# Picking expert outputs with a 0/1 product and combining on four row tiles, in a decoder layer on one core

## Time and profile before

| | us |
|---|---|
| median of 3 runs (2023.99 to 2030.28) | 2028.57 |
| the profiled execution | 2031.14 |
| its span, first to last instruction | 2029.3 |
| stage of experts in the trace, first DMA issue to first DMA issue of `combine` | 1841.07 to 1984.94 |
| `combine` in the trace, to the end of the span | 1984.94 to 2029.3 |
| busy over the whole span: PE / DVE / ACT / POOL | 87% / 63% / 42% / 27% |

### The profile page before, as it was taken

The page is one execution under the profiler, slowest core; times in us unless marked ns, Lnnn a source line. Parts: engine busy times, 40 slices in busy tenths (PEclk is TensorE's granted clock), DMA queues, the critical chain, the costliest instruction groups (busy, mean ns, idle before and its releaser), DMA issues. The chain is left out here.

```text
span 2029.3 us, 48825 instructions
## 1 busy us (share of the span) xinstructions
PE 1767.7 (87%) x19756; PEld 847.4 (42%) x19756; DVE 1268.6 (63%) x2435; ACT 858.0 (42%) x1031; POOL 543.2 (27%) x650
## 2 busy tenths in 40 slices
PE   3799999999998398999999989999999999976566
PEld 2556666666655222343343333333433333322224
DVE  4666666677663477867867777678678678821005
ACT  0333244333322114645645645545456546551213
POOL 0535455545512705014032041140140310000002
PEclk7899999999997669999999999999999999987775
DMA  5200000000000220211111201101111013145982
GB/s 180 81 24 3 24 24 24 3 24 24 3 13 3 64 96 2 70 45 45 38 36 49 69 1 62 56 25 48 45 49 48 22 49 131 75 176 211 421 372 97
DMA packets 64439, 143.62 MB, mean 71 GB/s; under 512 B 11376, under 2 KB 34448, under 8 KB 56048
## 3 DMA queue, kind: packets, MB, share of 16 engines
q1 hardware_dynamic: 59504, 136.29, 18.5%
q10 hardware_dynamic: 4736, 4.46, 0.7%
HBM read 97.59 MB, written 4.98 MB: 51 GB/s over the span
## 5 line engine op out<-in xcount | busy, mean ns | idle before, releaser
L1558 DVE TENSOR_REDUCE mx<-cpsV 128x1 f32<-128x512 f32 x1024 | 651.3, 684 | 228.0 <-PE cpsV L1261 214.1
L1462 ACT ACTIVATE w<-cpsA 128x1024 f32<-128x1024 f32 x512 | 496.2, 1021 | 373.7 <-PE cpsA L1329 373.6
L1261 PE MATMUL cpsV<-w 96*128 96x512 bf16 x1024 | 339.7, 403 | 63.2 <-DVE mx L1558 49.1
L1283 PE MATMUL cacc<-w 128*32 128x512 f32 x2048 | 281.1, 614 | 0.4 <-ACT w L1462 0.4
L1329 PE MATMUL cpsA<-w 99*128 99x512 bf16 x1024 | 276.9, 393 | 0.3
L1261 PEld LDWEIGHTS cpsV<-w 96*128 96x128 bf16 x1024 | 84.8, 99 | 376.9 <-DVE mx L1558 216.2
L1119 POOL TENSOR_TENSOR w<-w,zero 128x1024 bf16<-128x1024 f32 x21 | 39.7, 1892 | 645.1 <-ACTq L1435 645.1
L654 ACT COPY QK<-psA 128x1024 f32<-128x1024 f32 x64 | 64.8, 1012 | 252.2 <-PE psA L466 252.2
L1329 PEld LDWEIGHTS cpsA<-w 99*128 99x128 bf16 x1024 | 99.1, 100 | 128.2 <-ACT w L1462 11.8
L466 PE MATMUL psA<-xt,wq 128*128 128x512 f32 x256 | 133.3, 645 | 19.0 <-DMA xt<-in_xT 13.0
L744 POOL TENSOR_TENSOR VP<-V,VPF 128x128 f32<-128x128 f32 (+2 forms) x256 | 128.0, 531 | 45.7 <-PE psA L479 41.2
(11 more groups left out here) (214 smaller groups left out, 2396.5 us busy)
## 6 DMA issues: line engine op xcount, KB each, us to landing
w<-in_w SPq DMA_DIRECT2D x64, 1024.0 KB, 17.9
w<-w SPq DMA_DIRECT2D x192, 128.0 KB, 2.3
w<-w SPq DMA_DIRECT2D x192, 64.0 KB, 2.0
w<-in_ctxT SPq DMA_DIRECT2D x8, 1024.0 KB, 5.0
pro_xt<-in_xT SPq DMA_DIRECT2D x8, 512.0 KB, 7.0
x_tok<-in_x SPq DMA_DIRECT2D x8, 512.0 KB, 9.1
xtv<-in_xT SPq DMA_DIRECT2D x8, 512.0 KB, 5.0
xt<-in_xT SPq DMA_DIRECT2D x8, 512.0 KB, 4.5
```

What stands on the lines that cost most here:

```text
L1261: nc.tensor.matmul(out, Qst[q // 2][0:ROWS, hh, g * P:(g + 1) * P], Kst[q // 2][0:ROWS, hh, half * BANK:(half + 1) * BANK], start=True, st ...
L1283: last = nc.tensor.matmul(acc[BLK * jj:BLK * (jj + 1), :], Vc[:, c, 4 * q + jj, :], Pr[:, (2 * s + jj // 2) % 4, (jj % 2) * T:(jj % 2 + 1) ...
L1462: nc.scalar.activation(Pr[:, (2 * s + pp) % 4, :], src, ACT.Exp, scale=CA_SCALE).then_inc(act_evac, 1)
L1558: nc.vector.tensor_reduce(mx[:, q % 2, row, k % 2:k % 2 + 1], full(m[k]), AX_X, ALU.max).then_inc(dve_evac, 1)
```

## The change

`experts` and `combine` become one stage, `experts_and_combine`, written out without hardware loops. Weights, products, Gelu and the order inside a group stay; what differs:

1. `o_scratch` is gone, and so are the four DMAs per group, ACT's wait for them, the reload of `oall` and the barrier between the stages. Instead PE picks the rows: after the w1 product of group n it computes `pick_rows(n-1)`, eight products of a 0/1 table (`pick`, a new input of 128 x 480 fp32) with `og` of the group before, contraction over 128 partitions, 32 x 256 outputs each, accumulated over all groups in bank 7 (`psS`). Row tile j gets sequences j and 4+j, experts in partitions 32j to 32j+31.
2. DVE adds b2 from `psS` into `oall` (two instructions of 128 x 256) after the last pick.
3. The combination runs in 16 units of 256 tokens (half a sequence, one PSUM bank each), four units per `combine(s)`: eight products with 32 contraction rows, the four of one `g` in the four row tiles 0, 32, 64, 96 and in four banks.
4. For six of the units (`X_BY_PE`) PE first writes the tokens into the bank by a product with the identity (`add_x`), DVE only takes statistics from PSUM, and ACT normalizes straight from PSUM. Two of these `add_x` stand before the w2 product of the last group, four between `combine(1)` and `combine(2)`. For the other ten units DVE adds the tokens as before.
5. b1, `pick`, four copies of b2 and all eight p8 tiles are loaded at the stage's start, 14 DMAs in all; before its first w1 product PE waits for `c_loaded`, that is for `pick` and the four b2 copies, the last of which is the twelfth DMA in SP's order.
6. The w2 weights of the last group come in eight DMAs of half size, and its product waits for each half apart.
7. The output of all units has its own place in SBUF, over the first w1 buffer; SP issues the 16 output DMAs, two units at a time.

```diff
-def experts(nc, sh, dram):
+UNITS = 2 * B
+BT = 4
+def pick_table():
+    q, c = np.arange(P)[:, None, None], np.arange(2 * E - EG)[None, None, :]
+    b = np.arange(B)[None, :, None]
+    return ((q % BLK == b) & (c == E - EG + q // BLK)).astype(np.float32).reshape(P, -1)
+def experts_and_combine(nc, sh, dram, out):
...
+        psB, psS = ps[:, 5, :], ps[:, 7, :]
+        UNIT_BANKS = (5, 6, 0, 1), (2, 3, 4, 7)
+        def unit(u):
+            return BT * (u // 8) + u % BT, u // BT % 2, ps[:, UNIT_BANKS[u // BT % 2][u % BT], :]
+        X_BY_PE = (0, 1, 8, 9, 10, 11)
         @block.sync
         def _(sp):
             sp.dma_start(b1r[:], dram["w1"][:, D, :]).then_inc(b_loaded, 16)
-            sp.dma_start(sh.b2[:], dram["w2"][:, F, :]).then_inc(sh.b2_loaded, 16)
...
+            sp.dma_start(pick[:].rearrange("p b c -> p (b c)"), dram["pick"]).then_inc(c_loaded, 16)
+            for j in range(BT):
+                rows = slice(E * j, E * (j + 1))
+                sp.dma_start(b2[rows], dram["w2"][:, F, :]).then_inc(c_loaded, 16)
+                for h in range(2):
+                    t0 = (BT * h + j) * T
+                    sp.dma_start(p8[rows, h, :], sh.p8_dram[:, t0:t0 + T]).then_inc(p_loaded, 16)
+            for n in range(2, GROUPS):
+                sp.wait_ge(h_full, n - 1)
+                load_group_weights(sp, sh, dram, 1, n % 2, n * EG)
+                sp.wait_ge(o_full, n - 1)
+                if n < GROUPS - 1:
+                    load_group_weights(sp, sh, dram, 2, n % 2, n * EG)
+            for c0 in range(2):
...
+                    sp.dma_start(w2[n % 2][:, j, cs, :], src[:, cs, :]).then_inc(w2_part[c0], 16)
+            for u in range(UNITS):
+                sp.wait_ge(y_ready, u // 2 + 1)
+                sp.dma_start(out[b]...[:, 2 * half:2 * half + 2, :], y[:, u]).then_inc(saved, 16)
         @block.tensor
+            def pick_rows(n):
+                pe.wait_ge(o_evac, n + 1)
+                for h in range(2):
+                    for j in range(BT):
+                        last = nc.tensor.matmul(psS[E * j:E * (j + 1), h * D:(h + 1) * D],
+                                                pick[:, BT * h + j, E - EG - EG * n:2 * E - EG - EG * n], og[n % 2][:], ...)
+            def add_x(u):
+                for g in range(2):
+                    nc.tensor.matmul(bank[:, g * D:(g + 1) * D], sh.ident[:], sh.x[:, G * b + 2 * half + g, :], ...)
+            def combine(s):
+                for g in range(2):
+                    for j in range(BT):
+                        last = nc.tensor.matmul(bank[:, g * D:(g + 1) * D], p8[rows, b // BT, t0:t0 + P], oall[rows, b // BT, :], ...)
+            pe.wait_ge(c_loaded, 16 * (1 + BT))
+            for n in range(GROUPS):
+                (w1 product)
+                if n:
+                    pick_rows(n - 1)
+                (transposes)
+                if n == GROUPS - 1:
+                    for u in (0, 1):
+                        add_x(u)
+                (w2 product; in the last group waiting for w2_part[0], then w2_part[1])
+            pick_rows(GROUPS - 1)
+            combine(0)
+            combine(1)
+            for u in (10, 11, 8, 9):
+                (wait until unit u - 8 is out of the bank)
+                add_x(u)
+            combine(2)
+            combine(3)
         @block.scalar
-                    act.drain().then_inc(o_evac, 1)
-                    for j in range(EG):
-                        act.dma_start(sh.o_dram[...], og[n][BLK * j:BLK * j + B, :]).then_inc(o_saved, 16)
-                    act.wait_ge(o_saved, it * 128 + (n * 64 + 64 + 32))
+                if n >= 2:
+                    act.wait_ge(picked, n - 1)
+                nc.scalar.copy(og[n % 2][:], psO[n % 2]).then_inc(o_evac, 1)
         @block.vector
+            for h in range(2):
+                nc.vector.tensor_tensor(oall[:, h, :], psS[:, h * D:(h + 1) * D], b2[:], ALU.add).then_inc(oall_ready, 1)
+            for u in range(UNITS):
+                if u not in X_BY_PE:
+                    nc.vector.tensor_tensor(y[:, u], src, sh.x[...], ALU.add).then_inc(summed, 1)
+                dve.drain()
+                (2 bn_stats, drain, 2 bn_aggr)
```

More of the change, by code:

```diff
@@ L1672, in experts @@
         w2 = [t[:].rearrange("p (e c d) -> p e c d", e=EG, c=FC) for t in sh.w2]
+        y = sh.w1[0][:].rearrange("p (u g d) -> p u g d", u=UNITS, g=2)
         b1r, b1T = sb("b1r", [E, F]), sb("b1T", [P, FC, E])
@@ L1707, in _ @@
             pool.drain().then_inc(zeroed, 1)
[L1708 to L1713, removed]
+            for n in range(GROUPS):
+                if n >= 2:
+                    pool.wait_ge(h_full, n - 1)
+                nc.gpsimd.tensor_copy(mg4[n % 2][:, :, :, 0:B], sh.mT[:, :, EG * n:EG * (n + 1), :]).then_inc(mg_ready, 1)
@@ new lines, in add_x @@
+            def add_x(u):
+                b, half, bank = unit(u)
+                for g in range(2):
+                    nc.tensor.matmul(bank[:, g * D:(g + 1) * D], sh.ident[:], sh.x[:, G * b + 2 * half + g, :],
+                                     start=(g == 0), stop=False, skip_group_check=True)
+            def combine(s):
+                for g in range(2):
+                    for j in range(BT):
+                        u = BT * s + j
+                        b, half, bank = unit(u)
+                        t0, rows = (2 * half + g) * P, slice(E * j, E * (j + 1))
+                        last = nc.tensor.matmul(bank[:, g * D:(g + 1) * D], p8[rows, b // BT, t0:t0 + P], oall[rows, b // BT, :],
+                                                start=(u not in X_BY_PE), stop=True, skip_group_check=True)
+                last.then_inc(full, 1)
@@ new lines, in _ @@
+            for v in range(UNITS // 2):
+                act.wait_ge(rstd_ready, v + 1)
+                for u in (2 * v, 2 * v + 1):
+                    _, _, bank = unit(u)
+                    for g in range(2):
+                        src = bank[:, g * D:(g + 1) * D] if u in X_BY_PE else y[:, u, g, :]
+                        at = 2 * u + g
+                        last = nc.scalar.activation(y[:, u, g, :], src, ACT.Identity, bias=shift[:, at:at + 1],
+                                                    scale=rstd[:, at:at + 1])
+                last.then_inc(y_ready, 1)
@@ new lines, in _ @@
+            for u in range(UNITS):
+                b, half, bank = unit(u)
+                if u % BT == 0:
+                    dve.wait_ge(full, u // BT + 1)
+                src = bank.rearrange("p (g d) -> p g d", g=2)
+                if u not in X_BY_PE:
+                    nc.vector.tensor_tensor(y[:, u], src, sh.x[:, G * b + 2 * half:G * b + 2 * half + 2, :], ALU.add
+                                            ).then_inc(summed, 1)
+                    src = y[:, u]
+                dve.drain()
+                for g in range(2):
+                    nc.vector.bn_stats(stats[:, g, :], src[:, g, :])
+                dve.drain()
+                for g in range(2):
+                    last = nc.vector.bn_aggr(mv[:, u, g, :], stats[:, g, :])
+                if u % 2:
+                    last.then_inc(var, 1)
@@ L1917, in decoder_layer @@
             cross_attention(nc, sh, dram)
-            sh.b2 = weights.enter_context(nc.sbuf_tensor("b2", [E, D], F32))
-            sh.p8 = [weights.enter_context(nc.sbuf_tensor(f"p8_{n}", [E, T], F32)) for n in range(2)]
-            sh.b2_loaded = weights.enter_context(nc.semaphore("b2_loaded"))
-            sh.p8_loaded = [weights.enter_context(nc.semaphore(f"p8_loaded_{n}")) for n in range(2)]
-            experts(nc, sh, dram)
-            combine(nc, sh, dram, out)
+            experts_and_combine(nc, sh, dram, out)
 def _heads_inner(w):
```

245 lines of the change are left out of this document (91 added, 154 removed).

## The result

| | before | changed |
|---|---|---|
| median, us | 2028.8 (4 runs) | 2013.28 (4 runs, 2010.51 to 2016.96) |
| ratio, 95% interval | | 0.9929 (0.9905 to 0.9953) |
| forecast | | 2018.8, range 2012 to 2028 |
| profiled span | 2029.3 | 2008.8 |
| the stage: first DMA issue of the experts to the end of the span | 188.2 | 176.2 |

The changed kernel is faster by 15.5 us in the medians, more than the 9.8 us forecast. The two profiles differ by 20.5 us, but 8.5 of them lie ahead of the stage, in code that the change does not touch: the first DMA of the experts is issued at 1841.07 before and at 1832.61 after. It is 12.0 us shorter.

What follows compares the result with a forecast made beforehand. The weight stream bounds the experts, chains over engines the combination. End 1983.5 + 3.3 + 24.9 + 7.9 = 2019.5 against 2029.3, -9.8 us; from the median 2028.57 that gives 2018.8 us, range 2012 to 2028.

Steps and rivals of the forecast that it cites:

- rival D: Start costs little and PE stays hot: start +2, last group 11.6 us, -14.5 us in all, 2014.1 us; 16%.
- late start of the stream: At the stage's start PE's first w1 product waits for the twelfth DMA, moving the whole weight stream by 4.0 us.
- DVE's units: In the combination, ten units with an addition at 1.83 us, six without at 1.10: 24.9 us instead of 29.7.
- tail: After DVE's last unit, POOL, ACT and the output DMAs take 7.9 us, as before.
- Groups 0 to 6 at zero: DRAM wait goes, 16 short pick instructions per group come; both lie under the weight stream: 0 us.
- Group 7: Last group, from landing of w1 to end of w2 product: 14.3 us against 16.05, w1 product cold at 6.3.
- Half-size w2 at zero: Last group's half-size w2 transfers end four us before the second half is read: 0 us unless below half rate.
- Way to the first unit: From the last w2 product through og copy, picks, b2 addition and combine(0): 3.25 us instead of 10.4.
- Combine steps: Four row tiles overlap: sixteen instructions of combine(s) take 1.3 us first and 2 later, when PE is colder.
- Rival A: Row tiles do not run side by side: each combine(s) costs 7.0 us, PE bounds the end, 2034.6 us; 7%.
- B: Cold last group and late start eat the gain: start +5, last group 18 us, combine(2) late by 2, 2025.5; 22%.
- C: Late instruction fetch under the full stream, in the last group or the combination, costs 6 us: 2024.8 us; 10%.

Runs made afterwards that it cites:

- defer_c: Changed kernel with PE's wait for the table and b2 moved from ahead of the first w1 product to the first pick; stage 172.8 us, ratio 0.9899.
- before_lag: Kernel before, ACT's wait for the four DMAs to DRAM moved ahead of the copy that overwrites the same og buffer; stage 187.5 us, ratio 0.9996.
- scratch_writes: Changed kernel with the 32 small DMAs of og rows to DRAM put back beside the picks, read by nobody; stage 176.3 us, ratio 0.9942.
- warm2: Changed kernel with ten idle products on PE during its wait for the last w1 weights; stage 174.6 us, ratio 0.9931.
- whole_w2b: Changed kernel with the last group's w2 in four whole transfers, PE waiting for all; stage 176.2 us, ratio 0.9914.
- dram_trip: Changed kernel without the picks: og goes through DRAM and four DMAs bring it back, no barrier; stage 182.7 us, ratio 0.9950.
- x_by_dve: Changed kernel with X_BY_PE empty, so DVE adds the tokens for all 16 units; stage 179.1 us, ratio 0.9945.
- one_tile: Changed kernel with all combination products taking their rows from partitions 0 to 31, one row tile; stage 183.2 us, ratio 0.9967.

## Why the prediction was right

The mechanism held; the size, 12.0 us in the stage against 9.8, was off by the sum of small terms. In the median it is 15.5 against 9.8, and that the time came out so close to the range's lower end (2013.28, range from 2012), nearer to rival D's 2014.1 than to the forecast, is due to the stages that nobody changed and no merit of D. By its steps:

| step | predicted | measured |
|---|---|---|
| late start of the stream | +4.0 | +3.4 (9.88 to 13.27) |
| landing of the last w1 weights | +4.0 | +2.3 (124.1 to 126.5) |
| from there to the end of the w2 product, 16.05 before | 14.3 | 13.85 |
| from there to the first unit, 10.4 before | 3.3 | 3.56 |
| DVE's units, 29.7 before | 24.9 | 24.69 |
| tail, 7.9 before | 7.9 | 7.64 |
| stage | -9.8 | -12.0 |

- *Late start.* Right in mechanism, and shown by defer_c; 0.6 us too dear: 0.2 ahead of PE's start, 0.3 in the w1 product (6.24 us, where I had put 6.5), 0.1 between its end and SP's next issue.
- *Groups 0 to 6 at zero.* This was the term most off. The wait itself is hidden (before_lag), but the 32 small writes are not free for the stream: 512 packets, 0.7% of the DMA time of 135 us. Without them the stream took 1.1 us less from its start to the landing of the last w1 weights, and scratch_writes puts 1.0 back. I counted ACT's wait and forgot the transfer.
- *Group 7.* Cold w1 product 6.23 (predicted 6.3), transposes 1.16 (1.16), add_x 1.89 (2.0), w2 product 3.66 (3.66). The cause of the cold product, idleness ahead of it, is shown by warm2.
- *Half-size w2 at zero.* Right in value (whole_w2b), but with far less room than I thought: I had the stream end at 1972.0 in the kernel before, four us ahead of the reading of the second half after the change, by a flat 422 GB/s. In that trace the last weights landed 134.2 us into the stage, at 1975.2. In the changed kernel the stream falls to 193 and 98 GB/s in its last two us and ends at 136.4, and the product starts at 136.6.
- *Way to the first unit.* 3.56 against 3.25 (the terms named there add up to 3.2): the last picks took 1.07 us where I had 0.9, and from their end to PE's first combine step it was 0.7 us where I had 0.5. dram_trip has the way through DRAM at 10.1 with the new combination and without the barrier; of the gain over the kernel before, 4.1 us lie in that way.
- *Combine steps.* Taken at 1.3 and 2, measured 1.0 to 1.15, since the clock was at 1.00 in all four. It was not so between them: it stood at 0.50 from 1981.4 to 1984.8, in add_x, and was back in time for the third step. In x_by_dve, where no add_x runs, the third and fourth steps were at 0.50 and took 2.09 us each, near the 2 that I had put. DVE never waited for PE after the first unit.

Rival A is refuted by the steps of 1.0 to 1.15 us in the changed kernel. one_tile shows what A would have cost: 183.2 us, still 5.0 below before; A's price of 7.0 per step held for neither pair (5.6 and 4.2 us a step), since the clock was at 1.00 for part of both. Of B, the late start was there at 3.4 us in place of 5; its 18 us for the last group, cold until the middle of the w2 product, was not: the group took 13.85, cold in the w1 product alone, as the forecast had it. C did not show: eight instruction fetches, 0.13 MB in all, ran beside the full stream, and the last group's steps took no longer than their rows of before. That agrees with what the Trainium skill (Runtime: NRT & Kernel Launch, Instruction fetch mechanics) says of sequential fetching. D was right about neither: the start cost 3.4 and the product was cold.

Some 3 us of the measured 15 lie in stages that nobody changed, and no run here explains them.

## What to carry to other kernels

When a stage is bound by one continuous DMA stream, the only instructions that count in it are those ahead of the stream's start, those behind its end, and every byte added to it: a constant that is first needed later must not be waited for ahead of the work that releases the stream. What such a stage hides makes PE idle, and a PE that had been idle for 6.2 us was at a clock of 0.50 here at the very moment when the stream ended and PE became the path; a few dummy products, or real ones moved there, buy the clock back. Cross partitions with a product against a 0/1 table rather than through DRAM where the receiver waits: from the end of the og copy to DVE's addition it took 1.3 us here, in place of 5.3 in the kernel before and 6.9 in dram_trip.

## What the runs showed of the hardware that I had not expected

- PE's clock fell from 1.00 to 0.50 while PE was busy without a gap, in products of one row tile of 32 (one_tile), and it stayed at 0.50 through 28 us of such products before. In the changed kernel the same products spread over four row tiles ran at 1.00, but for 2.0 us at most at a stretch, and one_tile's ran at 1.00 for their first 2.8 us too. The contrast is in dram_trip: there the four-tile products started at 0.50 after an idle stretch, and the clock was back at 1.00 as they ended, 3.8 us later. One run with one such stretch shows this, and no run holds four row tiles busy for longer.
- Four row tiles at the same clock gave four times the pace of one, in fp32 with 128-column weights, and 3.2 times over a step of sixteen instructions.
- Written out, the eight groups hold one ACT_TABLE_LOAD of 1.28 us, ahead of the first Gelu; in the hardware loop there were eight, two per iteration. The stream hid them in both.
- The stream's end is not sharp: 193 GB/s and then 98 GB/s in the last two microseconds of the changed kernel, after 397.
